# Gated FFN of a two-layer model: integers turned as 16-bit halves of f32 numbers, x turned in pairs of tiles, and part of the rounding and of the gate product on POOL

## The reference

```
scale = 127 / clip(max|xn| per token)           xq = round(xn * scale)
gate  = (xq @ wq_gate) / scales                 up = (xq @ wq_up) / scales       # 256 -> 1024
h     = silu(gate) * up                         hq = round(h * 127 / clip(max|h| per token))
x     = x + tanh(g) * (hq @ wq_down) / scales                                    # 1024 -> 256
```

## Time and profile before

| | us |
|---|---|
| median of 3 runs (1500.18 to 1504.02) | 1500.19 |
| the profiled execution | 1502.58 |
| its span | 1500.8 |
| DVE, PE, ACT, POOL busy in the whole span | 1182.6, 1335.3, 1076.6, 729.9 |
| first gate matmul of the FFN, and start of its last `add` | 775.43 and 1046.59 |

### The profile page before, as it was taken

One profiled execution on the slowest core, in us unless ns is written; L12 is line 12 of the kernel. 1 busy time (PEld: TensorE's weight loads), 2 busy tenths in 40 slices (PEclk: granted clock), 3 DMA queues, 4 the chain that ended last, 5 costly groups with the idle time before them and its releaser, 6 DMA issues. The chain is left out here.

```text
span 1500.8 us, 30949 instructions
## 1 busy us (share of the span) xinstructions
PE 1335.3 (89%) x11612; PEld 904.7 (60%) x11612; DVE 1182.6 (79%) x1964; ACT 1076.6 (72%) x1810; POOL 729.9 (49%) x1154
## 2 busy tenths in 40 slices
PE   4799999999999999999978999996899986377686
PEld 3566666666666666666645666665667665133374
DVE  4478888788788788877768999985547999799775
ACT  2377777777777777777747888886455655699996
POOL 2156766757676576676665333421126667521000
PEclk9999999999999999999979999999899889599899
DMA  8655866866676685675310000000544442187399
GB/s 165 114 102 102 154 103 116 140 108 130 114 136 114 123 135 99 111 129 99 89 30 1 1 1 1 1 1 19 185 129 116 128 117 65 39 333 305 130 403 365
DMA packets 126469, 178.31 MB, mean 119 GB/s; under 512 B 47586, under 2 KB 78434, under 8 KB 120162
## 3 DMA queue, kind: packets, MB, share of 16 engines
q1 hardware_dynamic: 126032, 176.32, 49.6%
q10 hardware_dynamic: 288, 0.00, 0.0%
HBM read 82.36 MB, written 41.94 MB: 83 GB/s over the span
## 5 line engine op out<-in xcount | busy, mean ns | idle before, releaser
L735 DVE TENSOR_REDUCE neg_max<-psum 128x8 f32<-128x1024 f32 x256 | 313.2, 1223 | 70.4 <-PE psum L544 65.7
L672 ACT ACTIVATE exp_t<-psum 128x512 f32<-128x512 f32 x512 | 281.6, 597 | 49.3 <-PE psum L557 49.1
L838 POOL TENSOR_TENSOR rs<-rs,minus_half 128x16 f32<-128x16 f32 x64 | 186.3, 2912 | 5.0
L557 PEld LDWEIGHTS psum<-q_stack,k_stack 50*128 50x128 f32 x2048 | 137.5, 192 | 78.5 <-issue 75.2
L557 PE MATMUL psum<-q_stack,k_stack 50*128 50x128 f32 x2048 | 173.6, 290 | 0.8 <-ACT exp_t L672 0.8
L568 PE MATMUL psum<-exp_t,v_pad 128*32 128x256 f32 x2048 | 167.6, 400 | 0.0
L677 ACT ACTIVATE o_t<-psum 128x512 f32<-128x512 f32 x128 | 76.5, 598 | 95.6 <-PE psum L568 95.3
L544 PE MATMUL psum<-k_stack,q_stack 48*128 48x256 f32 x1024 | 136.1, 345 | 6.9 <-DVE neg_max L735 6.4
L943 PE MATMUL psum<-f_w,f_xqt 128*128 128x512 bf16 x512 | 125.1, 387 | 5.1 <-DVE f_hid L1071 5.0
L830 POOL TENSOR_TENSOR sq<-u 128x256 f32<-128x256 f32 x64 | 39.2, 612 | 175.7 <-DVE u L752 174.8
L544 PEld LDWEIGHTS psum<-k_stack,q_stack 48*128 48x128 f32 x1024 | 82.6, 193 | 55.8 <-issue 44.3
(11 more groups left out here) (220 smaller groups left out, 3050.4 us busy)
## 6 DMA issues: line engine op xcount, KB each, us to landing
k_stack<-k_hi SPq DMA_DIRECT2D x256, 128.0 KB, 4.6
g_scratch<-f_gelu SPq DMA_DIRECT2D x24, 1024.0 KB, 3.9
f_gelu<-g_scratch SPq DMA_DIRECT2D x24, 1024.0 KB, 14.9
k_stack<-k_lo SPq DMA_DIRECT2D x128, 128.0 KB, 4.7
ctx_t<-in_ctx_t SPq DMA_DIRECT2D x32, 256.0 KB, 5.3
x_state<-in_x SPq DMA_DIRECT2D x16, 512.0 KB, 6.6
v_in<-in_ctx SPq DMA_DIRECT2D x32, 256.0 KB, 5.7
v_scratch<-v_in SPq DMA_DIRECT2D x32, 256.0 KB, 5.0
```

What stands on the lines that cost most here:

```text
L557: r = e.matmul(psum[:, 2 + j, o:o + P], self.k_st[rows, b // 2 % self.NK, pair // 2 % 2, pair % 2, i, pair // 4, b % 2, :], self.q_st[rows ...
L672: e.activation(self.prob[:, n % 3, j].rearrange("p n w t -> p (n w t)"), psum[:, 2 + j, :], ACT.Exp).then_inc(s["exp"], 1)
L735: e.tensor_reduce(self.negm[:, b % 2, :, :, 2 * u:2 * u + 2].rearrange("p j w n -> p j n w"), psum[:, 0:2, :].rearrange("p j (n w k) -> p ...
L838: e.tensor_tensor(self.rs[:, i], self.rs[:, i], self.expo[:, :], ALU.pow).then_inc(s["pool"], 1)
```

## The change

1. The constant that is added in rounding becomes 1.5 * 2^23 + 2^14, so that the low 16 bits of the f32 number, read as an integer, are 2^14 plus the wanted integer (and, read as bf16, are never a special number). `turn_x` and `turn_h` transpose these low halves as bf16, with an identity matrix of bf16 (made once on POOL), and ACT reads the turned halves as int16 and takes 2^14 off.
2. A turned tile of h now takes one PSUM bank in place of two; tiles take the two banks in turn, and `turn_h(b)` waits for the conversion of tile b-2, not b-1.
3. x is turned and converted in pairs of tiles, at every even step: four transposes, and one ACT instruction of 128x512. `f_xqt` holds four tiles.
4. For odd tiles 5 to 59 (28 of them) `requantise` runs on POOL, not on ACT.
5. For tiles 4, 8, ..., 56 (14 of them) DVE's `hidden` is replaced by two steps: ACT copies up times its scale from PSUM to SBUF (`up_copied`), and POOL multiplies it by the silu in place (`product`). DVE takes the maximum of such a tile one step later.
6. POOL's statistics for the next stage (`sh.finish(w, 2, ...)`) move from steps b = 17, 25, ... to 19, 27, ...
7. Some semaphores of the weights are merged, which changes no order of instructions.

```diff
-    for h in range(2):
-        r = e.transpose(psum[:, 6, h * P:(h + 1) * P], self.xr[:, b % self.XR, h * P:(h + 1) * P], sh.ident[:, :])
+    out = psum[:, 6, j % 2 * 256:j % 2 * 256 + 256].bitcast(BF16)
+    for i in range(2):
+        for h in range(2):
+            r = e.transpose(out[:, (2 * i + h) * P:(2 * i + h + 1) * P],
+                            self.low(self.xr[:, (2 * j + i) % self.XR, h * P:(h + 1) * P]), self.ident16[:, :])
...
-            w.wait_ge(s["ht_sb"], b)
+            w.wait_ge(s["ht_sb"], b - 1)
+            out = psum[:, 4 + b % 2, :].bitcast(BF16)
             for i in range(self.NHT):
-                r = e.transpose(psum[:, 4 + i // 4, i % 4 * P:(i % 4 + 1) * P], self.hr[:, b % 2, i * P:(i + 1) * P], sh.ident[:, :])
+                r = e.transpose(out[:, i * P:(i + 1) * P], self.low(self.hr[:, b % 2, i * P:(i + 1) * P]), self.ident16[:, :])
...
+    def low(self, ap):
+        return ap.bitcast(BF16).rearrange("p (n two) -> p n two", two=2)[:, :, 0]
+    def product_on_pool(self, b):
+        return b % 4 == 0 and 4 <= b < NSEQ - 4
+    def rounded_on_pool(self, b):
+        return b % 2 == 1 and 4 <= b < NSEQ - 4
...
+        def up_copied(b):
+            w.wait_ge(s["up_pe"], b + 1)
+            self.hr_made(w, b - self.HS + 1)
+            e.activation(self.hid[:, b % self.HS], psum[:, 2:4, :].rearrange("p j c -> p (j c)"), ACT.Copy,
+                         scale=self.s_up[:, b:b + 1]).then_inc(s["up_sb"], 1)
...
             if 0 <= b < NSEQ:
-                hidden(b)
-                hidden_max(b)
+                if not self.product_on_pool(b):
+                    hidden(b)
+                if b > 0 and self.product_on_pool(b - 1):
+                    hidden_max(b - 1)
+                if not self.product_on_pool(b):
+                    hidden_max(b)
...
+        def product(b):
+            w.wait_ge(s["silu"], b + 1)
+            w.wait_ge(s["up_sb"], sum(self.product_on_pool(i) for i in range(b + 1)))
+            h = self.hid[:, b % self.HS]
+            e.tensor_tensor(h, h, self.gact[:, b % 2], ALU.mult).then_inc(s["hid_pool"], 1)
...
             if 0 <= b + 4 < NSEQ:
                 quantise(b + 4)
+            if 0 <= b - 1 < NSEQ and self.product_on_pool(b - 1):
+                product(b - 1)
+            if 0 <= b - 5 < NSEQ and self.rounded_on_pool(b - 5):
+                requantise(b - 5)
```

More of the change, by code:

```diff
@@ L239, in dve_sum @@
         w.wait_ge(self.s_load[i], 16)
-        w.e.tensor_reduce(self.sum[:, h, i:i + 1], self.half(self.w32, i, h), AX.X, ALU.add, apply_absolute_value=True).then_inc(self.s["sum"], 1)
+        w.e.tensor_reduce(self.sum[:, h, i:i + 1], self.half(self.w32, i, h), AX.X, ALU.add, apply_absolute_value=True).then_inc(self.s["dve"], 1)
     def act_sum_down(self, w, h):
@@ L252, in pe_means @@
         else:
-            w.wait_ge(self.s["sum"], 4)
+            w.wait_ge(self.s["dve"], self.SUMS)
             w.wait_ge(self.a0.s["max"], 4 * NSEQ)
@@ L888 @@
     H, NHT, HS = 1024, 8, 8
+    BASE = 2.0 ** 14
+    LOW = ROUND + BASE
     XR = 4
@@ L920, with up_read, hid_made, hr_made @@
     POOL_AHEAD = {62: range(-16, -11), 63: range(-11, -8), 64: range(-8, -1), 65: range(-1, 2), 67: range(2, 3)}
+    def low(self, ap):
[4 more added lines that the diff above has]
+        return b % 2 == 1 and 4 <= b < NSEQ - 4
+    def up_read(self, w, n):
+        on_pool = sum(self.product_on_pool(b) for b in range(n))
+        w.wait_ge(self.s["up_sb"], on_pool)
+        w.wait_ge(self.s["hid"], n - on_pool)
+    def hid_made(self, w, n):
+        on_pool = sum(self.product_on_pool(b) for b in range(n))
+        w.wait_ge(self.s["hid_pool"], on_pool)
+        w.wait_ge(self.s["hid"], n - on_pool)
+    def hr_made(self, w, n):
+        on_pool = sum(self.rounded_on_pool(b) for b in range(n))
+        w.wait_ge(self.s["hr_pool"], on_pool)
+        w.wait_ge(self.s["hr"], n - on_pool)
     def sp(self, w):
@@ L942, in project @@
                 for c in range(2):
-                    r = e.matmul(psum[:, bank + h, :], self.xqt[:, b % 2, c, :], weights[:, c, h * BANK:(h + 1) * BANK], start=c == 0, stop=c == 1)
+                    r = e.matmul(psum[:, bank + h, :], self.xqt[:, b % 4, c, :], weights[:, c, h * BANK:(h + 1) * BANK], start=c == 0, stop=c == 1)
             return r
         def gate_up(b):
-            w.wait_ge(s["xt_sb"], b + 1)
+            w.wait_ge(s["xt_sb"], b // 2 + 1)
             tw.wait_ready(w, 0)
@@ L978, in step @@
                 down(b - 7)
-            if 0 <= b + 2 < NSEQ:
-                turn_x(b + 2)
+            if b % 2 == 0 and 0 <= b + 2 < NSEQ:
+                turn_x((b + 2) // 2)
             if 0 <= b - 6 < NSEQ:
@@ L1028, in step @@
                 silu(b)
-            if 0 <= b - 5 < NSEQ:
+                if self.product_on_pool(b):
+                    up_copied(b)
+            if 0 <= b - 5 < NSEQ and not self.rounded_on_pool(b - 5):
                 requantise(b - 5)
-            if 0 <= b + 2 < NSEQ:
-                x_turned(b + 2)
+            if b % 2 == 0 and 0 <= b + 2 < NSEQ:
+                x_turned((b + 2) // 2)
             if b in (0, 1):
@@ L1889, in pe @@
         w.wait_ge(s["prep"], self.X_MAX)
-        e.transpose(psum[0:1, 6, 0:P], m1[:, 0:1], sh.ident[:, :]).then_inc(s["pe"], 1)
+        e.transpose(psum[0:1, 6, 0:P], m1[:, 0:1], sh.ident[:, :]).then_inc(self.fw.s["pe"], 1)
         w.wait_ge(s["prep"], self.X_ROW)
-        e.matmul(psum[:, 6, 0:1], sh.ones[0:1, :], self.row[:, 0:1], start=True, stop=True).then_inc(s["pe"], 1)
+        e.matmul(psum[:, 6, 0:1], sh.ones[0:1, :], self.row[:, 0:1], start=True, stop=True).then_inc(self.fw.s["pe"], 1)
         for u in range(-8, self.NU):
@@ L1898, in pe @@
         w.wait_ge(s["prep"], self.G_MAX)
-        e.transpose(psum[0:1, 6, 0:P], m1[:, 0:1], sh.ident[:, :]).then_inc(s["pe"], 1)
+        e.transpose(psum[0:1, 6, 0:P], m1[:, 0:1], sh.ident[:, :]).then_inc(self.fw.s["pe"], 1)
         w.wait_ge(s["prep"], self.G_ROW)
-        e.matmul(psum[:, 6, 0:1], sh.ones[0:1, :], self.row[:, 1:2], start=True, stop=True).then_inc(s["pe"], 1)
+        e.matmul(psum[:, 6, 0:1], sh.ones[0:1, :], self.row[:, 1:2], start=True, stop=True).then_inc(self.fw.s["pe"], 1)
         for q in range(self.NU):
```

87 lines of the change are left out of this document (49 added, 38 removed).

## The result

The changed kernel takes 1524.93 us (median of 4 runs, 1519.18 to 1546.2) against 1502.11 (4 runs, 1500.18 to 1505.74) of the kernel before in the same session: a ratio of 1.0128, 95% interval 1.008 to 1.0177, so it is slower, by 1.3% or some 19 us (22.8 by the medians of all four runs). A second set of runs (label `a0_after`, the changed kernel as it is) gives 1523.22, ratio 1.0111 [1.0017, 1.0206]. The execution that was profiled first, 1546.2, ran at half clock (0.50) from 45 to 121 us, in the first attention, which the change doesn't touch; the ratio is taken without it, and the median of the other three is 1520.91. I therefore read the profile of `a0_after`, span 1512.9. These rows are the views of the earlier trace rows in it.

The account below looks back on a forecast made before the run. A two-step chain through `add` and `down`, nearly level with PE's work, was taken as the bound. Terms -2.1 + 10.9 + 9.0 - 2.6 + 0.6 = +15.8 us gave median 1516, likeliest case 1509 to 1525, wider range 1498 to 1530.

Parts of the forecast that it names:

- Steady chain: Gated FFN, steps 9 to 57: 30.58 us per eight steps against 30.93, so 2.1 us less in six eights.
- The two legs: Four FFN steps as two chain parts: steps 3 to 1 (mod 4) 7.28 us, steps 1 to 3 8.01.
- bf16 turning: Turning x and h on PE: a bf16 128x128 transpose takes 0.055 us, half the 0.11 of f32.
- Late product: POOL's product for tiles 8, 16, ..., 48 makes the maximum 1.8 us late on the chain, six times: 10.9 us.
- Clock: PE's longer wait in those six places lowers the granted clock, 1.5 us each: nine in all.
- Late leg: Steps 1 to 3 (mod 4) with a late product: 8.01 us plus 1.8 for lateness and 1.5 for the clock.
- Tail: After step 64, the chain of turning h, conversion and `down` shortens by 0.43 us in six steps: 2.6 less.
- Start: Around steps 4 to 8, a second maximum delays the clamps and a missing `hidden` gives back time: 0.6 us more.
- Waits of `down`: PE's `down` waits for `x_state` about 1.7 us in steps 6, 14, ... and 3.5 in steps 10, 18, .
- The rival in which DVE's relief is paid in full: DVE's total work bounds the FFN: 4.9 us less per eight steps, some 32 over the stage, 1468; chance 0.15.
- Rounding on POOL: nothing: POOL's rounding of odd tiles takes at most four times 0.49 us, has two steps of time, and costs nothing.

Follow-up runs that it names:

- e1: Changed kernel with POOL's product moved ahead of the three rows (scales and f_xr) that wait for DVE; 1503.22 us, ratio 1.0005 to the kernel before.
- e2: Changed kernel, product still late, with unused matmuls filling PE's wait (26 in steps 10, 18, ..., 50; 18 in step 64); 1507.06 us, ratio 1.0003.
- e3: Changed kernel without the product on POOL: DVE does `hidden` for all tiles, POOL still rounds odd tiles; 1491.6 us, ratio 0.9952 to the kernel before.
- e5: Changed kernel with the orders of e1 and e4 together; 1490.26 us, ratio 0.9882 to the kernel before.
- e10: e4 with each maximum waiting only for the maker of its own tile, product still late; 1496.43 us, ratio 0.9953 to the kernel before.
- e4: Changed kernel with DVE taking the maximum of POOL's tile after `add`, product still late; 1499.12 us, ratio 0.9949 to the kernel before.
- e6: Changed kernel with neither product nor rounding on POOL, keeping bf16 turning, two banks for h and pairs of x; 1488.82 us, ratio 0.9875.
- e7: e5 with PE running `down` after both turnings; 1481.99 us, ratio 0.9829 to the kernel before.
- e9: e6 with PE running `down` after both turnings, nothing on POOL; 1480.15 us, ratio 0.9837 to the kernel before.
- e11: e10 with PE running `down` after both turnings, product still late; 1480.83 us, ratio 0.9842 to the kernel before.

## Why the prediction was right

By its own steps, with the stage's +17.0 us in the profile against +15.8 predicted:

- **Steady chain, -2.1.** e1, in which neither a late product nor a fall of the clock is left in these steps, has 183.1 against 185.2: -2.1. The two legs were predicted as 7.28 and 8.01; in the changed kernel gates of odd steps lie 7.28 to 7.33 and 7.92 apart.
- **bf16 turning, 0.055 each.** In the changed kernel the eight matmuls of `turn_h` occupy PE for 0.45 us from one row's start to the next (881.60 to 882.05), 0.056 each. The Trainium skill (TensorE: Matmul & The Clock Gate, section Back-to-back issue gap) gives 81 ns for a matmul of 128 columns in a stream with weight loads; here the measurement decides for the smaller number.
- **Late product, 1.8 x 6, put down as 10.9.** The product takes 2.36 us (predicted 2.33). From the start of `down` in step 24 it runs from 4.56 to 6.91, predicted 4.58 to 6.91. The maximum waits 1.81, six times, 10.8 in all, and e2 against e1 prices it at 11.4. Tiles 4, 12, ... do not wait.
- **Clock, 1.5 x 6 = 9.0.** Five of the six places show the lower level; together 9.0 us (a0_after against e2). Four of the dips cost 1.4 to 1.6 each, as priced, and the first 2.8. That the sum is exact is luck: one dip fewer than predicted, and one nearly twice as dear because the clock stayed low twice as long (last section).
- **Late leg.** 8.01 + 1.8 + 1.5 = 11.3; measured 11.22 to 11.44 where the clock fell and 9.82 where it held.
- **Tail, -2.6.** -3.1 (47.3 to 44.2). But I had not priced what comes before it. `down` in step 64 waited 1.98 in the kernel before and waits 2.42 or 2.43 in every variant with cheaper turnings and the old order of PE, and behind that wait the clock fell in five of eight profiles (first profile of the changed kernel, e1, e3, e5, e10) and held in three (a0_after, e4, e6). The stage's end is 43.4 to 44.2 where it held and 45.3 to 51.4 where it fell. From the first profile of the changed kernel (51.4):

```profile
1064.41 1.03 PE L1011 MATMUL psum<-f_w_down,f_hqt 128*128 128x256 bf16 x8 [2.43 <-DVE x_state L1141]
...
1067.10 1.89 PE L1011 MATMUL psum<-f_w_down,f_hqt 128*128 128x256 bf16 x8 [1.12 <-ACT f_hqt L1072]
```

- **Start, +0.6.** Three profiles with the same code up to step 9 (the two of the changed kernel, and e2) give 40.5, 40.0 and 37.9 against 38.7: it scatters more than the term, and why is not shown. The term can be neither confirmed nor refuted.
- **Waits of `down`.** Predicted 1.7 in one step of four and 3.5 in its late form; measured 1.44 and 3.34. The other leg has one of 0.85 that I had not listed; it is inside the 7.28 of the leg.

The median came out 9 us above the 1516 that I gave (5 above without the long execution), inside the range. The stage accounts for 17 us of the 22.8 over the kernel before, and for 23.5 in the profile in which the clock fell in the tail too; that such tails fill the gap in the median is possible and not shown, since the other timed runs have no profile. So the mechanism and the stage's +17.0 are confirmed term by term, and the rest of the median is not.

The rival in which DVE's relief is paid in full falls: with the lateness mended, the work given to POOL changes the six eights by +0.2 us (e5 against e6), and with `down` last by +1.0 (e7 against e9). The chain of `add` and `down` was the limit of the changed kernel, as the prediction said. It is not far ahead of DVE: once the work on POOL is gone (e6), the two legs of each eight in which DVE also takes the maxima of x last 7.87 and 7.46 us and stay so when `down` moves (e9), while the other two go from 7.33 to 6.74. When it is shortened (e9), DVE does become the bound, at 98% busy, and yet e7, where POOL relieves it, is no faster. What bounds e7 I have not followed to the end; PE waits there for `hidden` in front of the up half (0.7 us at most), in steps in which DVE takes two maxima before its next `hidden`, and neither PE (144) nor DVE (140 of 156 us) is full. "Rounding on POOL: nothing" held in the changed kernel, where the small step of DVE that rounding can hold up took 0.17 to 0.21 us in eleven of its twelve places and 0.43 in one; in e3, where the two fall together, it would have been wrong by 2.6 us (e3 against e6, below).

## What to carry to other kernels

When an operation moves to an engine with slack, look at what stands ahead of it in that engine's program, and at whose wait counts it: the product came 1.8 us late behind three tiny instructions, and 20 us were to be had by moving it past them, or as well by letting `add` and the other tiles' maxima pass it. Price such a lateness twice, once for the chain and once for TensorE's clock behind the longer idle. And test each part of a bundle alone: here the new turning (cheaper transposes, second bank and pairs of x together) carries the whole gain and the work on POOL none, and an order on PE that the change didn't touch was worth 5 to 10 us in the six eights and some 7 in the tail.

## What the runs showed of the hardware

**A small VectorE instruction held up by POOL.** DVE's step on four numbers per partition, L1134, normally takes 0.17 us. In e3, where POOL rounds at that moment, it took 0.68:

```profile
911.49 1.12 POOL L1217 TENSOR_SCALAR f_hr<-f_hid,f_hscale 128x1024 f32<-128x1024 f32 x1
911.95 0.68 DVE L1134 TENSOR_SCALAR f_hmax<-f_hmax 128x4 f32<-128x4 f32 x1
```

It ends at 912.63, just when POOL's instruction ends (912.61). Five of the twelve from step 9 to 57 were so long (0.68 to 0.71), one in each eight but the last; without POOL's rounding (e6) all are 170 to 171 ns, as the durations of that line (shortest, median, longest) show:

```profile
L1134 DVE TENSOR_SCALAR f_hmax<-f_hmax x12: 170/170/171, 822.1 to 986.3; 128x4 f32<-128x4 f32 x12
```

Once per eight steps this costs 0.51 us, which is the whole difference of e3 and e6 (30.49 and 29.98 per eight); in the last eight, where none is long, they take 29.44 and 29.45. The long maxima (1.22) and the PSUM-reading steps of DVE beside the same POOL work kept their durations. The Trainium skill (SBUF — State Buffer, section Who interferes with whom) has this: a `tensor_scalar` of VectorE can enter a mode that needs the port pair shared with GpSimd and is then blocked until the other is done, and a reduce never is. The trace agrees, for an instruction of four elements too.

POOL's product does the same to L1115, DVE's step on eight numbers per partition ahead of the reciprocal. In e5, where the product stands ahead of the scales, it took 0.74 to 0.79 us in five of the six eights, and where nothing of POOL ran beside it 0.17:

```profile
866.40 2.35 POOL L1212 TENSOR_TENSOR f_hid<-f_hid,f_act 128x1024 f32<-128x1024 f32 x1 [1.46 <-ACT f_hid L1059]
...
868.04 0.74 DVE L1115 TENSOR_SCALAR f_amax<-f_amax 128x8 f32<-128x8 f32 x1
```

Both end at 868.75 to 868.78. In e1 and e7 the same step takes 0.26 to 0.31. So the better order on POOL has a price on DVE of its own; what it costs an eight isn't separated by any run.

**The clock behind waits of PE.** The length of the wait alone did not decide. Behind 3.34 to 3.36 us the granted clock fell to 0.50 in most places, but not in all (in both profiles of the changed kernel one of the six late steps kept 1.00). Behind 2.42 or 2.43 it fell in five profiles of eight. In e4 the same wait of 2.20 to 2.22 stands in six places; the clock fell behind two of them and held behind four, which the eight matmuls of `down` right behind show (1.23 and 1.12 us where it fell, 1.03 where not, as in the row with e4). The first of the two:

```profile
845.69 1.23 PE L1011 MATMUL psum<-f_w_down,f_hqt 128*128 128x256 bf16 x8 [2.21 <-DVE x_state L1141]
```

Shorter waits are no safe side either. `down` of step 64 waited 1.97 or 1.98 in five profiles; the clock held behind four and fell behind that of e11, in which the stretch right behind has 0.50:

```profile
1010.04 1.33 PE L1011 MATMUL psum<-f_w_down,f_hqt 128*128 128x256 bf16 x8 [1.97 <-DVE x_state L1145]
```

```profile
1011.00:1013.00 2.00, 2.00 (x15) 1.64 (x14) 0.82 (x2) 0.74 (x1) 1.68 (x6) 0.50 0.00 0
```

In steps 9 to 57 no wait of `down` of 1.51 or less was followed by a fall. What a fall costs goes with how long the clock stays low. Four of those in the changed kernel's steady part lasted some 3.5 us and cost 1.4 to 1.6; the first lasted nearly 7 and cost 2.8:

```profile
819.00:825.00 6.00, 5.12 (x25) 3.39 (x27) 3.98 (x7) 2.07 (x3) 5.26 (x14) 0.50 0.01 3
```

In the tail, where PE is half idle, it cost up to 7, in the profile in which the clock stayed low to the end of the stage (51.4 us against 44.2).
